# A linear-attention and FP4 feed-forward kernel: eight small adds and the final norm moved to ScalarE, and the turn's order rearranged on four engines

## The chip, the cores and the metric

One core of one Trainium2 chip runs the kernel. The metric is device time in microseconds (us), from launch to end; lower is better. Each kernel is run several times and its median counts. A profile of one execution gives the start and the length of every instruction on the engines: PE (TensorE), DVE (VectorE), ACT (ScalarE), POOL (GpSimd), and SP, the queue that issues the DMAs.

## The reference, cut to what matters

```
x = L0_attn_x                                  # (32, 256, 128), float32
q, k, v = (x @ W).reshape(b, s, 64, 64)        # for Wq, Wk, Wv
q = relu(q) * 64 ** -0.5 ;  k = relu(k)
kv  = einsum('bsid,bsjd->bsdj', k, v)
out = einsum('bsid,bsdj->bsij', q, kv)         # 64 x 64 for each token
out = out / (einsum('bsid,bsd->bsi', q, k.sum(axis=2)) + 1e-6)
x = layernorm(x + out.reshape(b, s, 4096) @ Wo + bo)
g, u = fp4_linear(x, w_gate), fp4_linear(x, w_up)
x = layernorm(x + fp4_linear(silu(g) * u, w_down))
# fp4_linear rounds both operands in blocks of 16 to the grid
# 0, .5, 1, 1.5, 2, 3, 4, 6, scaled by the block's largest magnitude over 6
```

The attention is within one token, across its 64 heads.

## The kernel before, in words

The 8192 tokens are cut into 64 tiles of 128. `run_tiles` runs 68 turns, and each turn works on five tiles at different stages: turn n projects v, k and q of tile n (`front`), attends for tile n-1 (`attend`), multiplies tile n-2 by Wo (`mid`), does the first layernorm, the gate and up products and the quantisation of tile n-3 (`back`), and the down product and the second layernorm of tile n-4 (`end`). Every float32 operand of a large matmul is split in two bfloat16 halves, "hi" (a rounded copy, made by ScalarE) and "lo" (what is left, made by VectorE or GpSimd), and each product takes three matmuls (`three`, lines 360 to 362).

The order of the work is written out by hand: each engine has an `iteration(t)`, a list of helpers, and runs its helpers strictly in that order. Between engines stand semaphores, which each helper waits for at its head. So a wait at the head of one helper holds up everything behind it on its engine. What the change touches:

- PE, one turn (lines 462 to 497): v in four chunks of 24 matmuls, a transpose of x, k in four chunks with the transpose of h (`h_transpose`, line 426) before the last, the down product (`down`, line 433, which waits for ScalarE's copy `hqT`), then q chunk 0, `out_group` 0, `k_sum` (line 444), `out_group` 1, the transpose of xq (line 451), gate and up (lines 459 and 460), q chunk 1, groups 2 and 3, q chunk 2, groups 4 and 5, two parts of Wo (line 407), q chunk 3, groups 6 and 7 with the rest of Wo. Chunks and groups share three slots of PSUM; each waits until the vector engine has read what was there before.
- `q_bd` is the block-diagonal form of q that the groups load as weights. It is filled by four DMAs (`q_move` on SP), three copies by ScalarE (`q_stay`, line 564, copies (l=1, a=0), (0, 1), (0, 0)) and one by GpSimd (`q_stay`, line 1096). Group 0 of the next turn waits for all of them. The part l=1 needs all four `q_lo` of the turn.
- The normaliser of a group is column 32 of its PSUM slot. VectorE adds 1e-6 (`norm_o`, line 774), takes the reciprocal (`recip`, line 781, for one or two groups) and multiplies (`scale_o`, line 790) into one of two buffers `o32`; ScalarE rounds that to `o_st` (`o_hi`, line 623), and GpSimd writes the rest (`o_lo`, line 1066). `scale_o(g)` waits for `o_lo(g-2)`. In the same way `q_scale` (line 766), `q_hi` (line 597) and `q_lo` (line 1056) handle q.
- The sum of k over the heads: ScalarE's `k_first`, VectorE's three `k_add` (line 731), then `k_fold` 0, 1 and 2 (line 742), which halve `k_acc` from 1024 to 128 columns, then PE's `k_sum` and ScalarE's `k_sums` (line 577).
- `y` (line 899) is the last layernorm's product on VectorE, (r2 - mean) * rstd; `rstd_2` on GpSimd gives the rstd. `h_back` (line 1115) multiplies the rounded h by its scales on GpSimd.
- `h_scale` (line 923) is a tensor_scalar on a small tile in SBUF, among the steps of the h quantisation on VectorE.

The weights are loaded and split before and in the first turns: `weight_hi` on ScalarE, the loop over "vkq" on VectorE (lines 706 to 715), and Wo's lo half on GpSimd (line 1046).

Of the kernel before, what the change touches and what calls it, by code (L numbers as in the profile page):

```python
# [28 lines left out]
ALU = mybir.AluOpType  # L29
# [3 lines left out]
P = 128  # L33
DIM = 128
# [3 lines left out]
T = 128  # L38
# [81 lines left out]
def attention_ffn(nc, x, wq, wk, wv, wo, bo, w_gate, w_up, w_down, out):  # L120
# [5 lines left out]
    with ctx:  # L126
        def sb(name, shape, dt=F32):
            return ctx.enter_context(nc.sbuf_tensor(name, shape, dt))
# [27 lines left out]
        consts = sb("consts", [P, 5])  # L156
# [10 lines left out]
        ve1, rs1, ve2, rs2 = (sb(v, [T, 1]) for v in ("ve1", "rs1", "ve2", "rs2"))  # L167
# [7 lines left out]
        def slot_cols(u):  # L175
# [46 lines left out]
         s_ve2, s_rs2, s_yo, s_store) = (sem(f"s_{v}") for v in (  # L222
             "hmax hsc hrs hn hm hk ht hs hq hps hqT dn x1b r2 st2 agg2 ve2 rs2 yo store").split())
# [34 lines left out]
        def _(sp):  # L258
# [34 lines left out]
            def iteration(t):  # L293
                if t.mid:
# [208 lines left out]
        def _(act):  # L503
# [16 lines left out]
            weight_hi("q")  # L520
# [85 lines left out]

            def h_step(t):
# [18 lines left out]
            def iteration(t):  # L626
                v_hi(t, 0)
                v_hi(t, 1)
                v_hi(t, 2)
                v_hi(t, 3)  # L630
# [4 lines left out]
                q_stay(t, 1, 0)  # L635
                hq_copy(t)
                q_stay(t, 0, 1)
                q_stay(t, 0, 0)
                k_sums(t)
                if t.is_(1):  # L640
                    down_weights()
                x1_keep(t)
                xq_copy(t)
# [25 lines left out]
        def _(dve):  # L669
# [3 lines left out]
            nc.vector.memset(consts[:, 4:5], 1.0)  # L673
            nc.vector.memset(consts[:, 1:2], EPS_LN).then_inc(s_consts, 1)
# [31 lines left out]
            for k in "vkq":  # L706
# [8 lines left out]
                last.then_inc(s_wlo[k], 1)  # L715

# [53 lines left out]

            def norm_o(t, g):
                if t.attend:
                    dve.wait_ge(s_done["out"], t.o * NG + g + 1)
                    nc.vector.tensor_scalar(nrm[:, g % NR, :], slot_cols(("out", g))[:, :, HALF], EPS_NORM, None,
                                            ALU.add).then_inc(s_nrm, 1)
# [175 lines left out]
            def iteration(t):  # L951
                residual_1(t)
                stats_1(t)
                before_mean_1(t)
                v_lo(t, 0)
                mean_1(t)
                v_lo(t, 1)
                v_lo(t, 2)
                x_one(t)
# [22 lines left out]
                norm_o(t, 1)  # L982
# [8 lines left out]
                norm_o(t, 2)  # L991
                norm_o(t, 3)
# [7 lines left out]
                norm_o(t, 4)  # L1000
                norm_o(t, 5)
# [3 lines left out]
                y(t)  # L1005
# [3 lines left out]
                norm_o(t, 6)  # L1009
                norm_o(t, 7)  # L1010
# [11 lines left out]
        def _(pool):  # L1022
# [21 lines left out]
            nc.gpsimd.memset(vst[1][:, 1, :, :, HALF:VS], 0.0).then_inc(s_clear, 1)  # L1044
            pool.wait_ge(s_whi["o"], 1)
# [34 lines left out]
            def rstd_2(t):  # L1080
                if t.end:
                    rstd(t.e, s_agg2, mv2, ve2, rs2, s_ve2, s_rs2)

            def q_stay(t):
# [78 lines left out]
```

## Time and profile before

| | us |
|---|---|
| runs of the kernel before | 2352.80, 2371.66, 2376.55 |
| their median | 2371.66 |
| the profiled execution: its own time | 2365.52 |
| its span, first to last instruction | 2363.7 |
| mean granted TensorE clock in it | 0.969 |

The span is what the engines' rows cover; some 2 us of the profiled time lie around it. Busy shares over the whole span are averages, so they mix the first turns, 60 steady turns and the last ones. The turn is the unit to read: one list of helpers on each engine.

### The profile page before, as it was taken

The numbers are of one execution on the slowest core, as the hardware profiler recorded it, in microseconds if no ns is written. First come the engines' busy times: TensorE is split into PE (matmuls) and PEld (weight loads), VectorE is DVE, ScalarE is ACT, GpSimd is POOL, SyncE is SP. The second block draws the span as 40 slices with busy tenths as digits, with TensorE's granted clock in tenths as the row PEclk, the third lists the DMA queues.
The fourth block names the chain that finished last, engine by engine and source line by source line (L and its number), as shares of the span: only waits on it lengthen the run. The fifth ranks groups of instructions, "written<-read, shape, count | busy, mean of one in ns | idle before, by whom it ended". The sixth has DMA issues, their size and how long they took to land.

```text
span 2363.7 us, 88235 instructions
## 1 busy us (share of the span) xinstructions
PE 2079.3 (88%) x37963; PEld 1977.0 (84%) x37963; DVE 1937.1 (82%) x3933; ACT 1489.2 (63%) x2634; POOL 1676.8 (71%) x2064
## 2 busy tenths in 40 slices
PE   3799999999898999999989999899889989989975
PEld 3788898888888888888888888889888888888864
DVE  7678888888888888888888888888888888888874
ACT  4566666666666666666666666666666666666651
POOL 3577787777677777777767767678667767767773
PEclk8899999999999999999999999999999999999986
DMA  6366656656655755665665665666665655655651
GB/s 186 83 132 148 135 129 136 147 125 130 148 121 123 152 126 120 149 134 115 147 135 113 147 129 118 148 129 129 138 132 116 147 126 121 148 128 120 147 119 39
DMA packets 523212, 308.29 MB, mean 130 GB/s; under 512 B 275590, under 2 KB 497734, under 8 KB 522310
## 3 DMA queue, kind: packets, MB, share of 16 engines
q1 hardware_dynamic: 522822, 302.65, 59.3%
q8 instruction: 298, 4.88, 0.8%
q14 instruction: 92, 0.75, 0.1%
HBM read 17.38 MB, written 4.19 MB: 9 GB/s over the span
## 4 chain that ended last, share of the span: by engine, by line
PE 46%; POOL 18%; ACT 16%; DVE 13%; issue 6%; DMA 1%; DVEq 0%; ACTq 0%; SPq 0%; POOLq 0%
PE ps L360 11%; ACT q_bd L564 11%; PE ps L362 10%; PE ps L361 10%; PE ps L407 10%; POOL o_st L1066 8%; POOL q_nat L1056 8%; DVE q L766 4%; DVE o L790 3%; ACT q_nat L597 2%; PE ps L444 1%; PE ps L459 1%; ACT hqT L571 1%; DVE v_st L749 1%; PE ps L426 1%
## 5 line engine op out<-in xcount | busy, mean ns | idle before, releaser
L1066 POOL TENSOR_TENSOR o_st<-o,o_st 128x256 bf16<-128x256 f32 x1024 | 662.8, 677 | 75.5 <-ACT o_st L623 73.7
L1056 POOL TENSOR_TENSOR q_nat<-q,q_nat 128x512 bf16<-128x512 f32 x512 | 591.1, 1176 | 60.3 <-ACT q_nat L597 60.1
L360 PE MATMUL ps<-v_st,q_bd 128*128 128x66 bf16 x4096 | 462.9, 200 | 139.5 <-ACT q_bd L564 73.4
L360 PEld LDWEIGHTS ps<-v_st,q_bd 128*128 128x128 bf16 x4096 | 421.3, 115 | 169.9 <-DVE o L790 85.4
L623 ACT CAST o_st<-o 128x256 bf16<-128x256 f32 x1024 | 356.6, 404 | 310.2 <-DVE o L790 308.1
L361 PE MATMUL ps<-v_st,q_bd 128*128 128x66 bf16 x4096 | 459.4, 199 | 0.0
L362 PE MATMUL ps<-v_st,q_bd 128*128 128x66 bf16 x4096 | 458.3, 198 | 0.0
L361 PEld LDWEIGHTS ps<-v_st,q_bd 128*128 128x128 bf16 x4096 | 421.7, 117 | 0.3 <-issue 0.2
L362 PEld LDWEIGHTS ps<-v_st,q_bd 128*128 128x128 bf16 x4096 | 420.1, 116 | 0.0
L597 ACT CAST q_nat<-q 128x512 bf16<-128x512 f32 x512 | 292.0, 617 | 179.0 <-DVE q L766 178.8
L749 DVE TENSOR_TENSOR v_st<-ps,v_st 128x1024 bf16<-128x1024 f32 x256 | 312.4, 1222 | 106.4 <-ACT v_st L540 99.4
L407 PE MATMUL ps<-w_o,o_st 128*128 128x128 bf16 x6144 | 376.2, 220 | 6.0 <-DMA o_st<-swap 6.0
L790 DVE TENSOR_TENSOR o<-ps,rec 128x512 f32<-128x512 f32 x512 | 342.6, 682 | 43.8 <-POOL o_st L1066 38.9
L360 PE MATMUL ps<-xT,w_v 128*128 128x128 bf16 x2048 | 352.1, 221 | 20.6 <-DVE v_st L749 14.6
L564 ACT COPY q_bd<-q_nat 64x2048 bf16<-64x2048 bf16 x192 | 363.5, 1893 | 7.8 <-POOL q_nat L1056 4.6
L360 PE MATMUL ps<-xT,w_q 128*128 128x128 bf16 x2048 | 360.2, 220 | 5.1 <-DVE q L766 5.0
L361 PE MATMUL ps<-xT,w_q 128*128 128x128 bf16 x2048 | 359.9, 220 | 0.0
L362 PE MATMUL ps<-xT,w_q 128*128 128x128 bf16 x2048 | 359.9, 220 | 0.0
L407 PEld LDWEIGHTS ps<-w_o,o_st 128*128 128x128 bf16 x6144 | 351.7, 114 | 7.0 <-DMA o_st<-swap 7.0
L360 PE MATMUL ps<-xT,w_k 128*128 128x128 bf16 x2048 | 352.0, 220 | 5.3 <-DVE v_st L749 5.3
L361 PE MATMUL ps<-xT,w_v 128*128 128x128 bf16 x2048 | 352.2, 221 | 0.0
L362 PE MATMUL ps<-xT,w_v 128*128 128x128 bf16 x2048 | 352.2, 221 | 0.0
(125 smaller groups left out, 5411.9 us busy)
## 6 DMA issues: line engine op xcount, KB each, us to landing
q_bd<-q_nat SPq DMA_DIRECT2D x256, 256.0 KB, 4.1
swap<-v_st SPq DMA_DIRECT2D x64, 576.0 KB, 6.4
v_st<-v_st SPq DMA_DIRECT2D x64, 576.0 KB, 5.3
v_st<-swap SPq DMA_DIRECT2D x64, 576.0 KB, 5.5
swap<-o_st SPq DMA_DIRECT2D x64, 512.0 KB, 4.3
o_st<-o_st SPq DMA_DIRECT2D x64, 512.0 KB, 8.4
o_st<-swap SPq DMA_DIRECT2D x64, 512.0 KB, 6.0
x_in<-in_L_attn_x SPq DMA_DIRECT2D x64, 64.0 KB, 5.6
```

Of the source, the lines that this page charges most:

```text
L360: nc.tensor.matmul(dst, lhs(0), rhs(0), start=True, stop=False)
L361: nc.tensor.matmul(dst, lhs(0), rhs(1), start=False, stop=False)
L362: return nc.tensor.matmul(dst, lhs(1), rhs(0), start=False, stop=True)
L407: last = nc.tensor.matmul(Y, omat[t.par][:, lo, j // EB, :, j % EB], womat[:, lw, j, :], start=(j == 0 and k == 0), stop=(j == HALF - 1 an ...
L564: nc.scalar.copy(qbd[rows, l, :, a, e:e + HALF, :].rearrange("p k e s -> p k (e s)"), qnat[rows, l, a].rearrange("p k e s -> p k (e s)")). ...
L597: last = nc.scalar.copy(qnat[:, 0, a, :, c * EC:(c + 1) * EC, :], src[:, a])
L623: last = nc.scalar.copy(ost[1 - t.par][:, 0, :, a, g * G:(g + 1) * G, :], src[:, a])
L749: nc.vector.tensor_tensor(lo, slot_cols(("v", c)).rearrange("p e t -> p t e"), hi, ALU.subtract).then_inc(s_read["v"], 1)
L766: nc.vector.scalar_tensor_tensor(out=q32[:, c % QR, :].rearrange("p (e t) -> p e t", t=T), in0=slot_cols(("q", c)), scalar=0.0, in1=ks[:, ...
L790: nc.vector.tensor_tensor(o32[:, g % OR, :].rearrange("p (s b e) -> p s b e", b=2, e=HALF), slot_cols(("out", g))[:, :, 0:PW].rearrange("p ...
L1056: last = nc.gpsimd.tensor_tensor(qnat[:, 1, a, :, e, :], src[:, a], qnat[:, 0, a, :, e, :], ALU.subtract)
L1066: last = nc.gpsimd.tensor_tensor(lo[:, :, a], src[:, a], hi[:, :, a], ALU.subtract)
```

## The change

It has these parts.

1. `norm_o`, eight per turn, goes from VectorE to ScalarE, as an activation with the 1e-6 as a per-partition bias taken from `consts`. It stands at nine places between ScalarE's copies, and waits there for PE's group and, because of the ring of four, for an earlier `recip`.
2. `y` goes from VectorE to ScalarE, as an activation with scale rstd and bias -mean * rstd. GpSimd works out that bias with two more instructions in `rstd_2`, one of which waits for the rstd. ScalarE does `y` before `q_hi(1)`.
3. On ScalarE the second `q_stay` copy goes ahead of `hq_copy`.
4. On VectorE `x_round` and `x_grid` close up around `k_fold(2)`, and `mean_1` goes ahead of `v_lo(0)`.
5. On GpSimd `q_lo(3)` goes ahead of `o_lo(6)` and `o_lo(7)`, `x_bias` ahead of `q_lo(2)`, and `h_back` from the end of turn n to the head of turn n+1, between `rstd_1` and `q_stay`. GpSimd's `q_stay` waits for `o_lo` and `h_back` too.
6. On SP the two `q_move(1, ...)` go ahead of the first move of `o_st`.
7. In the first turn the split of Wq goes behind the third chunk of v on ScalarE and VectorE, and GpSimd's lo half of Wo waits for the three folds (`s_tree` at 3).

The diff, cut to its core:

```
 # ScalarE
+def norm_o(t, g):
+    if not t.attend: return
+    if not (t.is_(1) and g < NR):
+        act.wait_ge(s_rec, t.o * NG + g + 1 - NR)
+    act.wait_ge(s_done["out"], t.o * NG + g + 1)
+    nc.scalar.activation(nrm[:, g % NR, :], slot_cols(("out", g))[:, :, HALF], ACT.Identity,
+                         bias=consts[:, 6:7]).then_inc(s_nrm, 1)
+def y(t):
+    if t.end:
+        act.wait_ge(s_store, 16 * (t.e + 1))
+        act.wait_ge(s_nb, t.e + 1)
+        nc.scalar.activation(y_out[:, :], r2[:, :], ACT.Identity, bias=nb[:, 0:1],
+                             scale=rs2[:, 0:1]).then_inc(s_yo, 1)
 ...
                 o_hi(t, 1)
+                norm_o(t, 2)
+                norm_o(t, 3)
+                y(t)
                 q_hi(t, 1)
 ...
                 o_hi(t, 5)
+                norm_o(t, 6)
                 q_hi(t, 3)
+                norm_o(t, 7)
                 o_hi(t, 6)
 # GpSimd
             def rstd_2(t):
                 if t.end:
                     rstd(t.e, s_agg2, mv2, ve2, rs2, s_ve2, s_rs2)
+                    nc.gpsimd.tensor_tensor(nm[:, :], mv2[:, 0:1], consts[:, 5:6], ALU.mult).then_inc(s_nm, 1)
+                    pool.wait_ge(s_rs2, t.e + 1)
+                    pool.wait_ge(s_nm, t.e + 1)
+                    nc.gpsimd.tensor_tensor(nb[:, :], nm[:, :], rs2[:, :], ALU.mult).then_inc(s_nb, 1)
 ...
                 rstd_1(t)
+                h_back(t)
                 q_stay(t)
 ...
+                x_bias(t)
                 q_lo(t, 2)
                 o_lo(t, 4)
                 o_lo(t, 5)
-                x_bias(t)
+                q_lo(t, 3)
                 o_lo(t, 6)
-                h_back(t)
                 o_lo(t, 7)
-                q_lo(t, 3)
 # GpSimd, before the turns
+            pool.wait_ge(s_tree, 3)
             pool.wait_ge(s_whi["o"], 1)
             nc.gpsimd.tensor_tensor(w_o[:, 1, :], stage["o"], w_o[:, 0, :], ALU.subtract).then_inc(s_wlo["o"], 1)
```

On ScalarE, this is the stretch from `k_first` to the copy of xqT in a steady turn, before. `q_bd<-q_nat` are the `q_stay` copies, `hqT<-ps` is `hq_copy`, `ks<-ps` is `k_sums`.

```order
L552 ACTIVATE k_acc<-ps 128x1024
L564 COPY q_bd<-q_nat 64x16x128
L571 COPY hqT<-ps 128x128 x2
L571 COPY hqT<-ps 96x128
L564 COPY q_bd<-q_nat 64x16x128 x2
L577 COPY ks<-ps 128x128
L582 COPY x1b<-x 128x128
L587 COPY xqT<-ps 128x128
```

And the same stretch in the changed kernel, where line 613 is `norm_o`:

```order
L552 ACTIVATE k_acc<-ps 128x1024
L564 COPY q_bd<-q_nat 64x16x128 x2
L571 COPY hqT<-ps 128x128 x2
L571 COPY hqT<-ps 96x128
L564 COPY q_bd<-q_nat 64x16x128
L613 ACTIVATE nrm<-ps,consts 128x8
L577 COPY ks<-ps 128x128
L582 COPY x1b<-x 128x128
L613 ACTIVATE nrm<-ps,consts 128x8
L587 COPY xqT<-ps 128x128
```

Two copies of q stand ahead of the copy of hqT now instead of one, and a norm ahead of ks and another ahead of xqT.

On VectorE, this is the stretch of the folds, before. `nrm<-ps` is `norm_o(0)`, `xq<-xm,xq` is `x_round`, `xq<-xq,xm` is `x_grid`.

```order
L742 TENSOR_TENSOR k_acc<-k_acc 128x512
L863 SCALAR_TENSOR_TENSOR xm<-xm,consts 128x128
L742 TENSOR_TENSOR k_acc<-k_acc 128x256
L774 TENSOR_SCALAR nrm<-ps 128x8
L742 TENSOR_TENSOR k_acc<-k_acc 128x128
L870 TENSOR_TENSOR xq<-xm,xq 128x128
L781 RECIPROCAL rec<-nrm 128x8
L875 TENSOR_TENSOR xq<-xq,xm 128x128
```

And in the changed kernel, where lines 774 and 807 are the fold and the reciprocal:

```order
L774 TENSOR_TENSOR k_acc<-k_acc 128x512
L889 SCALAR_TENSOR_TENSOR xm<-xm,consts 128x128
L774 TENSOR_TENSOR k_acc<-k_acc 128x256
L896 TENSOR_TENSOR xq<-xm,xq 128x128
L774 TENSOR_TENSOR k_acc<-k_acc 128x128
L901 TENSOR_TENSOR xq<-xq,xm 128x128
L807 RECIPROCAL rec<-nrm 128x8
```

The norm, which waits for group 0 on PE, no longer stands between the second and the third fold, and the first reciprocal comes behind the whole of the x quantisation.

## Rows read from the trace of the kernel before

**Rows 1.** Timeline of DVE, line 899: start, length, instruction; of 60 rows three.

```profile
202.50 0.70 DVE L899 SCALAR_TENSOR_TENSOR y_out<-r,mv,rs 128x128 f32<-128x128 f32 x1
...
1251.76 4.21 DVE L899 SCALAR_TENSOR_TENSOR y_out<-r,mv,rs 128x128 f32<-128x128 f32 x1
...
2282.14 0.67 DVE L899 SCALAR_TENSOR_TENSOR y_out<-r,mv,rs 128x128 f32<-128x128 f32 x1
```

**Rows 2.** Two turns from y to y: busy of PE, PEld, DVE, ACT, POOL; clock; DMA.

```profile
270.93:305.04 34.11, 31.62 (x597) 30.34 (x595) 28.61 (x63) 23.06 (x41) 25.91 (x33) 1.00 0.64 137
1251.76:1288.68 36.92, 32.59 (x586) 30.55 (x584) 31.67 (x62) 22.96 (x41) 25.92 (x33) 0.95 0.60 126
```

**Rows 3.** Timelines of POOL and PE beside the long y of rows 1.

```profile
1254.54 1.29 POOL L1066 TENSOR_TENSOR o_st<-o,o_st 128x256 bf16<-128x256 f32 x2
...
1256.63 0.22 PE L360 MATMUL ps<-v_st,q_bd 128*128 128x66 bf16 x1 [1.79 <-DVE o L790]
```

**Rows 4.** Timeline of PE in a short turn; in brackets the idle time before and its releaser.

```profile
287.80 0.89 PE L433 MATMUL ps<-w_dn,hqT 128*128 128x128 f32 x6
288.53 0.22 PE L360 MATMUL ps<-xT,w_q 128*128 128x128 bf16 x1
...
291.16 0.22 PE L360 MATMUL ps<-v_st,q_bd 128*128 128x66 bf16 x1 [1.12 <-ACT q_bd L564]
...
292.60 0.38 PE L444 MATMUL ps<-k_acc,both 128*128 128x128 f32 x1 [0.46 <-DVE k_acc L742]
...
294.48 0.54 PE L459 MATMUL ps<-w_gu,xqT 128*128 128x352 f32 x1 [0.45 <-ACT xqT L587]
...
300.49 0.22 PE L360 MATMUL ps<-v_st,q_bd 128*128 128x66 bf16 x1 [0.32 <-DVE o L790]
```

**Rows 5.** Timeline of ACT in the same turn.

```profile
284.57 1.88 ACT L564 COPY q_bd<-q_nat 64x2048 bf16<-64x2048 bf16 x1
286.67 0.59 ACT L571 COPY hqT<-ps 128x128 f32<-128x128 f32 x3 [0.21 <-PE ps L426]
287.28 3.82 ACT L564 COPY q_bd<-q_nat 64x2048 bf16<-64x2048 bf16 x2
```

**Rows 6.** Timeline of DVE in the same turn: the folds.

```profile
289.98 0.68 DVE L742 TENSOR_TENSOR k_acc<-k_acc 128x512 f32<-128x512 f32 x1
...
292.18 0.17 DVE L774 TENSOR_SCALAR nrm<-ps 128x8 f32<-128x8 f32 x1 [0.98 <-PE ps L362]
292.27 0.28 DVE L742 TENSOR_TENSOR k_acc<-k_acc 128x128 f32<-128x128 f32 x1
```

**Rows 7.** Groups by line: busy us, mean ns of one, idle before.

```profile
L774 DVE TENSOR_SCALAR nrm<-ps 128x8 f32<-128x8 f32 x512 | 68.5, 157 | 103.1 <-PE ps L362 103.1
L577 ACT COPY ks<-ps 128x128 f32<-128x128 f32 x64 | 17.1, 267 | 138.1 <-PE ps L444 138.1
L610 ACT ACTIVATE sig<-sig,consts 128x352 f32<-128x352 f32 x64 | 37.6, 587 | 7.0 <-DVE sig L798 7.0
```

**Rows 8.** Timelines of POOL and, last, DVE in the turn of rows 4.

```profile
294.89 0.19 POOL L1072 TENSOR_TENSOR ve<-mv,consts 128x1 f32<-128x1 f32 x1 [1.26 <-DVE mv L893]
...
295.95 2.31 POOL L1056 TENSOR_TENSOR q_nat<-q,q_nat 128x512 bf16<-128x512 f32 x2 [0.24 <-ACT q_nat L597]
298.22 2.56 POOL L1066 TENSOR_TENSOR o_st<-o,o_st 128x256 bf16<-128x256 f32 x4
...
300.88 0.69 DVE L790 TENSOR_TENSOR o<-ps,rec 128x512 f32<-128x512 f32 x1 [0.44 <-POOL o_st L1066]
```

**Rows 9.** The first turn: timelines of POOL, DVE and PE.

```profile
42.64 7.93 POOL L1046 TENSOR_TENSOR w_o<-o_st,w_o 128x4096 bf16<-128x4096 f32 x1 [10.06 <-ACT w_o L523]
...
43.31 8.59 DVE L742 TENSOR_TENSOR k_acc<-k_acc 128x512 f32<-128x512 f32 x3
...
51.95 0.58 PE L444 MATMUL ps<-k_acc,both 128*128 128x128 f32 x1 [8.60 <-DVE k_acc L742]
```

**Rows 10.** Line 923 (`h_scale`): lengths in ns, least, median, greatest.

```profile
L923 DVE TENSOR_SCALAR hsc<-hsc x64: 168/570/716, 162.3 to 2352.1; 128x22 f32<-128x22 f32 x64
```

More of the change, by code:

```diff
@@ L166, in attention_ffn @@
         mv1, mv2 = sb("mv1", [T, 2]), sb("mv2", [T, 2])
-        ve1, rs1, ve2, rs2 = (sb(v, [T, 1]) for v in ("ve1", "rs1", "ve2", "rs2"))
+        small = sb("small", [T, 6])
+        ve1, rs1, ve2, rs2, nm, nb = (small[:, i:i + 1] for i in range(6))
         ps = ctx.enter_context(nc.psum_tensor("ps", [P, 8, 512], F32))
@@ L221, in attention_ffn @@
         (s_hmax, s_hsc, s_hrs, s_hn, s_hm, s_hk, s_ht, s_hs, s_hq, s_hps, s_hqT, s_dn, s_x1b, s_r2, s_st2, s_agg2,
-         s_ve2, s_rs2, s_yo, s_store) = (sem(f"s_{v}") for v in (
-             "hmax hsc hrs hn hm hk ht hs hq hps hqT dn x1b r2 st2 agg2 ve2 rs2 yo store").split())
+         s_ve2, s_rs2, s_nm, s_nb, s_yo, s_store) = (sem(f"s_{v}") for v in (
+             "hmax hsc hrs hn hm hk ht hs hq hps hqT dn x1b r2 st2 agg2 ve2 rs2 nm nb yo store").split())
         PER = {"k": NC - 1, "v": NC, "q": NC, "out": NG}
@@ L293, in iteration @@
             def iteration(t):
+                if t.attend:
+                    sp.wait_ge(s_qlo, (t.n * NC))
+                    q_move(1, 0)
+                    q_move(1, 1)
                 if t.mid:
@@ L605, in sigmoid @@
                     nc.scalar.activation(sig[:, :], TB0[:, 0:FFN], ACT.Sigmoid).then_inc(s_sig, 1)
+            def norm_o(t, g):
+                if not t.attend:
+                    return
+                if not (t.is_(1) and g < NR):
[3 more added lines that the diff above has]
+                                     bias=consts[:, 6:7]).then_inc(s_nrm, 1)
             def h_step(t):
@@ L629, in iteration @@
                 v_hi(t, 2)
+                if t.is_(0):
+                    weight_hi("q")
                 v_hi(t, 3)
@@ L635, in iteration @@
                 q_stay(t, 1, 0)
+                q_stay(t, 0, 1)
                 hq_copy(t)
-                q_stay(t, 0, 1)
                 q_stay(t, 0, 0)
+                norm_o(t, 0)
                 k_sums(t)
@@ L642, in iteration @@
                 x1_keep(t)
+                norm_o(t, 1)
                 xq_copy(t)
@@ L650, in iteration @@
                 o_hi(t, 3)
+                norm_o(t, 4)
+                norm_o(t, 5)
                 q_hi(t, 2)
@@ L704, in _, with weight_lo @@
             nc.vector.tensor_tensor(xT[0][:, 1, :], TB1[:, 0:T], xT[0][:, 0, :], ALU.subtract).then_inc(s_xlo, 1)
-            for k in "vkq":
+            def weight_lo(k):
                 dve.wait_ge(s_whi[k], 1)
@@ L715, in _ @@
                 last.then_inc(s_wlo[k], 1)
+            weight_lo("v")
+            weight_lo("k")
             def down_quantise():
@@ L769, in q_scale @@
                 ).then_inc(s_read["q"], 1)
[L771 to L775, printed above, removed]
             def recip(t, g, count):
@@ L954, in iteration @@
                 before_mean_1(t)
+                mean_1(t)
                 v_lo(t, 0)
-                mean_1(t)
                 v_lo(t, 1)
                 v_lo(t, 2)
+                if t.is_(0):
+                    weight_lo("q")
                 x_one(t)
@@ L973, in iteration @@
                 k_fold(t, 1)
-                norm_o(t, 0)
+                x_round(t)
                 k_fold(t, 2)
-                x_round(t)
+                x_grid(t)
                 recip(t, 0, 1)
-                x_grid(t)
                 stats_2(t)
@@ L1091, in q_stay @@
                 pool.wait_ge(s_qlo, t.n * NC)
+                if t.mid:
+                    pool.wait_ge(s_olo, t.o * NG)
                 if t.back:
-                    pool.wait_ge(s_rs1, t.b + 1)
                     pool.wait_ge(s_x1, t.b + 1)
+                if t.end:
+                    pool.wait_ge(s_hq, t.e + 1)
                 held = qnat[64:128, 1, 1].rearrange("p k e s -> p k (e s)")
@@ L1112, in h_back @@
             def h_back(t):
-                if t.back:
-                    pool.wait_ge(s_hs, t.b + 1)
+                if t.end:
+                    pool.wait_ge(s_hs, t.e + 1)
                     nc.gpsimd.tensor_tensor(blocks(h[:, :]), blocks(h[:, :]), per_block(hsc[:, 0, :], h[:, :]),
```

24 lines of the change are left out of this document (3 added, 21 removed).

## The prediction, as made before the changed kernel ran

> **What bounds the kernel now.** I first listed the starts of one instruction that runs once a turn, y on VectorE. From the first of rows 1 to the last there are 60 of them and 59 intervals: 2282.14 - 202.50 = 2079.6 us, 35.25 each. They are of three kinds, by the length of y. It is near 0.70 us in most turns and 4.2 us in 20 of them [rows 1]. The 20 intervals with a long y at their head average 36.92 us, the 19 behind such a one 34.58, the other 20 34.21; the least is 34.11. (20 x 36.92 + 19 x 34.58 + 20 x 34.21 is 2079.6.) So of 2079.6 us only 59 x 34.11 = 2012.5 are quiet turns, and 67 us hang on the long y or on what follows it.
>
> What the long y waits for is to be seen beside it: y ran from 1251.76 to 1255.97, GpSimd was at work until 1255.83, and y ended 0.14 us after that [rows 1, 3]. It reads r2 and rstd, both in SBUF. Meanwhile group 7's slot was not read and PE stood for 1.79 us [rows 3]. Such a turn also shows a granted clock of 0.95 against 1.00 in the quiet one [rows 2]: after the standstill some of PE's work ran at 1.2 in place of 2.4 GHz.
>
> Then a quiet turn, 34.11 us, in which PE is busy 31.62, VectorE 28.61, GpSimd 25.91 and ScalarE 23.06 [rows 2]. PE's timeline shows what it stands for: 1.12 us for ScalarE's last copy of q_bd, 0.46 for the third fold, 0.45 for xqT, and 0.32 for scale_o(2) [rows 4]; scale_o(3) is late too, since it starts as o_lo(1) of GpSimd ends (300.78, then 300.88) [rows 8]. So PE bounds the turn, with some 2.5 us of short waits in it, and VectorE's own busy time matters only where it is late.
>
> **The change, part by part, in a quiet turn.**
>
> *hq_copy behind the second q_stay.* PE's down product needs hqT. Now it starts at 287.80, and group 0 waits for the last q_stay, which ends at 291.10 [rows 4, 5]. In the new order the copies run at 284.57 and, at the pitch of a pair (3.82 - 1.89 = 1.93), 286.50, to 288.39. hqT follows to 289.02, and the third q_stay to 290.95. PE's down would start at about 289.1, q chunk 0 0.73 later, group 0 another 24 x 0.0556 = 1.34 later: 291.17, where it stood at 291.16. The wait moves from q_bd to hqT and is worth nothing; bounds +0.1, and -0.2 where ScalarE had waited for h's transpose (0.21 us here). I take 0.
>
> *The fold.* The third fold started at 292.27, behind a norm that had waited 0.98 us for group 0 [rows 6]. Without it the chain is set by the down product: its end at 289.99, residual_2 to 290.3, first fold from 290.45, third over at about 292.1. Group 0's issue ends at 291.97, so k_sum starts at 292.13, where it was 292.60: -0.47. The wait of 0.46 [rows 4] is nearly gone. Bounds -0.2 and -0.6. x_grid is over earlier as well, so xq is not late next.
>
> *Norms on ScalarE.* On VectorE one took 157 ns [rows 7]. The nearest rows on ScalarE are a PSUM copy of 128 columns without a per-partition operand, 267 ns, and h_step with one, 587 ns for 352 columns [rows 7]. I take 0.27, bounds 0.2 and 0.4. Eight are 2.2 us of ScalarE a turn and y about 0.5 (bounds 0.3 and 0.6): 23.06 becomes 25.8, which has room. What matters is the place. norm_o(1) waits for group 1 and stands ahead of the copy of xqT; PE's transpose of xq ends only a little behind group 1, so the copy is late by a quarter to a half of a norm: +0.07. norm_o(3) waits for group 3 and with y stands ahead of q_hi(1), which starts about 0.9 late against PE. But its follower q_lo(1) on GpSimd stands behind o_lo(1) anyway [rows 8], by my walk with 0.2 us to spare: 0, and if that cover is gone 0.2 to 0.5. The other norms replace a VectorE step of the same wait: 0.
>
> The Trainium skill speaks against this part. "ScalarE: Activation LUTs", in its rules for kernel authors, gives adds and multiplies to VectorE rather than ScalarE, and under "What ACT_TABLE_LOAD costs" it gives 186 ns, plus 93 for each per-partition operand, plus 0.833 ns a column. By that a norm is 286 ns and y 479 ns. The engine with fewer waits on it is here the better place in spite of the rule, by the rows above, since what goes is a wait on VectorE and not work.
>
> *nm and nb.* Two more instructions of 0.19 us, with a wait, stand ahead of q_lo(0). GpSimd had waited 0.24 us there for q_hi(0) [rows 8]. The rstd starts 0.07 earlier, as a norm is gone ahead of mean_2. Net +0.09 (bounds 0 and +0.25).
>
> *What of it reaches the end of the turn.* PE comes to gate and up 0.47 - 0.07 = 0.40 earlier. Later it waits for scale_o(2) and (3), and (3) hangs on GpSimd: q_lo(0) is 0.47 - 0.09 = 0.38 earlier, and so are o_lo(1) and group 5. Behind that nothing waits long. So a quiet turn is 34.11 - 0.38, say 33.75 us.
>
> *GpSimd's order.* Its work between q_lo(0) and q_stay is the same in sum once nm and nb are counted before it. By my walk through the turn rstd_1 is over 0.8 us before x_one, and h_back ends as x_one starts. x_one reads two SBUF operands, like y; if it is held, it is for at most the 0.8 us of h_back, and PE then waits at k chunk 2. I take 0, bound +0.3 a turn. o_st's first move goes out over a microsecond later, behind q_move(1, ...) on SP, but Wo, which waits for the third one, did not wait in a steady turn. q_move(1, ...) goes out earlier, off the path. mean_1 is off it too.
>
> *y off VectorE.* No instruction that stands long at the meeting with GpSimd is left but h_scale, below. The 20 long turns and the turns behind them become quiet ones. The 20 intervals with no long y near them still averaged 34.21, 0.10 over the least; I keep that. So 59 x (35.25 - 33.85) = 82.6 us less, of which 61 are y and 21 the shorter turn.
>
> *The first turn.* The three folds took 8.59 us beside Wo's lo half (7.93 us on GpSimd), and PE stood 8.60 [rows 9]. Undisturbed, the first and the third take 0.68 and 0.28 [rows 6] and the middle one lies between, 1.4 in all, so 7.2 go. Wq's split no longer stands ahead of v_lo, which puts the folds some 2 us earlier, but then Wo's lo half stands ahead of q_lo(0), and q_scale(2) waits for that. I take -8, bounds -4 and -10. The three or so turns before 202.50 give -1, and the longer chain to the last y +0.5.
>
> **The sum** is made against the profiled execution, 2365.5: 2365.5 - 82.6 - 8 - 1 + 0.5 = 2274.4. That execution is 6 us below the median of the runs, 2371.66. The runs differ by 24 us, which is some 8 long turns, so I expect the changed kernel's runs to lie closer together, and its median where its profile is: **2275 us**, -4.1%.
>
> The page "GPSIMD Engine Reference" of the Trainium skill says in its key points that GpSimd shares its SBUF interfaces with VectorE and contends with VectorE instructions that read two SBUF operands or use a two-port mode. The trace agrees for y (up to 4.2 us), for the folds (8.59 against 1.4 us) and for h_scale (0.57 against 0.17).
>
> **The rivals.**
>
> *Only y counts.* If the norm ahead of xqT, nb, or q_hi(1) eat what the fold gives back, the quiet turn stays at 34.11: 59 x (35.25 - 34.21) = 61, so 2365.5 - 61 - 8 = 2296. For it: PE's waits are chained, and one that goes has often an heir. Against: the fold's 0.46 is followed by nothing as tight but 0.09 of GpSimd.
>
> *The short waits go altogether.* If GpSimd's q_lo(0) moves with the fold and the copy of hqT is quicker than I have it, another 0.4 us a turn: 2275 - 24 = 2251. Against: o_lo(1) is limited by GpSimd's own work.
>
> *h_scale takes y's place (slower).* It is a tensor_scalar from SBUF to SBUF, and it took 570 ns in the median where its least is 168 [rows 10]: it already waits 0.4 us for GpSimd each turn, but has always been let in at the next end of a GpSimd instruction, as y was in two turns of three. With the norms gone from ahead of it, it meets o_lo(0) about 0.05 us later in GpSimd's phase. If it is let in as badly as y, a turn costs 2.8 us (36.92 - 34.11), and scale_o(2) is held behind it. The change's gain of 91 us is used up from 91 / 2.8 = 32 long turns of 59; with all 59 it would be 2275 + 165 = 2440. Against: 0.716 us is its greatest in 64 turns.
>
> *The norms' place.* If ScalarE's queue is late by 0.5 us at q_hi(1) in each turn, and GpSimd with it: 2275 + 30 = 2305.
>
> **Chances.** Forecast (2255 to 2290) 0.52. Only y, or the norms late (2290 to 2348) 0.27. The short waits gone (below 2255) 0.10. h_scale or another meeting with GpSimd 0.11, of which 0.05 ends within 1% of before and 0.06 above. The measurement tells about 1% from no change. So faster 0.89, same 0.05, slower 0.06. The range reaches from the third case to the end of the second's mass: 2245 to 2325.
>
> **What the profile of the changed kernel would show.** Right: turns of 33.6 to 34.0 us with hardly a spread; PE waiting about 1.1 us for hqT at the down product, next to nothing for q_bd and under 0.2 for the fold; o_lo(1) still ahead of group 5; norms near 0.27 us; the first k_sum at about 42 us instead of 51.95. Wrong: turns of 34.1 (a wait took the fold's place; its row would have a releaser on ScalarE or GpSimd), or 33.3 (GpSimd did not hold group 5), or a VectorE instruction of 3 to 4 us on h_scale, x_one or a fold.

## The result, and the profile after

The changed kernel takes 2272.06 us (median of 4, 2269.25 to 2275.05), the kernel before beside it 2373.8 (median of 4, 2352.8 to 2376.55). The ratio is 0.959, interval 0.954 to 0.964. (Ratios, here and below, leave out a kernel's runs that lie more than 1.5% above its fastest.) The forecast was 2275 us, in a range of 2245 to 2325. The profiled execution took 2271.46 us; its span is 2269.7 where it was 2363.7, so 94.0 us went.

Where they went is read first from one instruction that runs once a turn on VectorE, residual_1. This is its source view, before and then after (form, least/median/longest in ns, first and last start).

```profile
L811 DVE TENSOR_TENSOR r<-ps,x_res x64: 278/279/292, 141.1 to 2342.1; 128x128 f32<-128x128 f32 x64
```

```profile
L837 DVE TENSOR_TENSOR r<-ps,x_res x64: 278/281/293, 133.4 to 2245.0; 128x128 f32<-128x128 f32 x64
```

Ahead of the first one 141.1 - 133.4 = 7.7 us are gone. The 63 intervals between took 2201.0 and take 2111.6: 89.4 less. Behind the last one 21.6 us became 24.7: 3.1 more. The sum is 94.0. The intervals of the steady part are 33.5 to 34.2 us, three in four of them between 33.65 and 33.85, and none is long. One such turn in the view by windows (busy of PE, PEld, DVE, ACT, POOL; clock), to be held against the two of [rows 2]:

```profile
1212.73:1246.50 33.77, 31.65 (x597) 30.38 (x595) 27.59 (x53) 25.02 (x52) 26.11 (x35) 1.00 0.65 138
```

PE's work is the same 31.6 us. Nine instructions per turn (eight norms and y) went from VectorE to ScalarE; the counts in the rows differ by one or two more, from instructions cut by the windows' edges. VectorE is busy 1.0 us less than in the quiet turn before, ScalarE 2.0 more. It is 2.0 and not the 2.7 forecast, since an instruction on ScalarE partly overlaps its neighbour in the records. The granted clock is 1.00, with no dip; from 200 to 2180 us it averages 1.00 too, where the kernel before had 0.99.

PE's timeline of the same turn answers to [rows 4] (in brackets the idle time before, and its releaser):

```profile
1225.14 0.94 PE L434 MATMUL ps<-w_dn,hqT 128*128 128x128 f32 x6 [1.08 <-ACT hqT L571]
1225.92 0.22 PE L361 MATMUL ps<-xT,w_q 128*128 128x128 bf16 x1
...
1227.26 0.19 PE L361 MATMUL ps<-v_st,q_bd 128*128 128x66 bf16 x1
...
1228.21 0.38 PE L445 MATMUL ps<-k_acc,both 128*128 128x128 f32 x1
...
1230.16 0.53 PE L460 MATMUL ps<-w_gu,xqT 128*128 128x352 f32 x1 [0.52 <-ACT xqT L587]
...
1236.22 0.22 PE L361 MATMUL ps<-v_st,q_bd 128*128 128x66 bf16 x1 [0.36 <-DVE o L816]
```

Measured from the start of v in the turn, 1212.73 here and 276.63 in [rows 4]:

| PE reaches | before | forecast | after |
|---|---|---|---|
| down product | 11.17 | 12.47 | 12.41 |
| group 0 | 14.53 | 14.54 | 14.53 |
| k_sum | 15.97 | 15.50 | 15.48 |
| gate and up | 17.85 | 17.45 | 17.43 |
| group 4 | 23.86 | not given | 23.49 |
| end of the turn | 34.11 | 33.75 | 33.77 |

The 1.12 us for q_bd became 1.08 for hqT, and the 0.46 for the fold is gone. VectorE in this stretch, against [rows 6]:

```profile
1226.53 0.68 DVE L774 TENSOR_TENSOR k_acc<-k_acc 128x512 f32<-128x512 f32 x1
...
1227.33 0.42 DVE L774 TENSOR_TENSOR k_acc<-k_acc 128x256 f32<-128x256 f32 x1
...
1227.87 0.28 DVE L774 TENSOR_TENSOR k_acc<-k_acc 128x128 f32<-128x128 f32 x1
```

The third fold ends at 1228.15, 0.06 ahead of k_sum. GpSimd at its meeting with q, against [rows 8]:

```profile
1230.42 0.19 POOL L1084 TENSOR_TENSOR small<-mv,consts 128x1 f32<-128x1 f32 x1 [1.52 <-DVE mv L919]
1230.69 0.55 POOL L1086 TENSOR_TENSOR small<-small,consts 128x1 f32<-128x1 f32 x1
1231.21 0.19 POOL L1095 TENSOR_TENSOR small<-mv,consts 128x1 f32<-128x1 f32 x1
1231.55 0.19 POOL L1098 TENSOR_TENSOR small<-small 128x1 f32<-128x1 f32 x1
1231.69 2.30 POOL L1068 TENSOR_TENSOR q_nat<-q,q_nat 128x512 bf16<-128x512 f32 x2
1233.95 2.57 POOL L1078 TENSOR_TENSOR o_st<-o,o_st 128x256 bf16<-128x256 f32 x4
```

Lines 1095 and 1098 are nm and nb. From q_scale(0) to q_lo(0) it was 2.52 us and is 2.66. Measured from the start of v again, q_scale(0) starts at 16.30 us instead of 16.80, q_lo(0) at 18.96 instead of 19.32, and scale_o(3), which waits for o_lo(1), at 23.89 instead of 24.25: 0.36 us earlier, where the forecast had 0.38. The other row to remember is the first: GpSimd sat idle for 1.52 us ahead of rstd_2, and from there it has no gap of size until the end of the turn.

The two operations that moved to ScalarE, and h_scale, the one that could have taken y's place, in their source views:

```profile
L613 ACT ACTIVATE nrm<-ps,consts x512: 253/267/270, 82.6 to 2218.6; 128x8 f32<-128x8 f32 x171
...
L626 ACT ACTIVATE y_out<-r,small x64: 481/483/493, 187.5 to 2267.2; 128x128 f32<-128x128 f32 x64
...
L941 DVE TENSOR_SCALAR hsc<-hsc x64: 178/637/700, 153.8 to 2257.3; 128x22 f32<-128x22 f32 x64
```

y now takes 0.48 us each time. h_scale still waits for GpSimd in nearly every turn, and never for more than 0.70 us.

The first turn answers to [rows 9]:

```profile
41.96 1.48 DVE L774 TENSOR_TENSOR k_acc<-k_acc 128x512 f32<-128x512 f32 x3
44.32 1.22 DVE L798 SCALAR_TENSOR_TENSOR q<-ps,ks 128x1024 f32<-128x1024 f32 x1 [0.88 <-ACT ks L577]
...
53.80 1.23 DVE L798 SCALAR_TENSOR_TENSOR q<-ps,ks 128x1024 f32<-128x1024 f32 x1 [5.42 <-POOL q_nat L1068]
```

The three folds take 1.48 us, and the first k_sum starts at 43.49 us; it had been 51.95, and the forecast was about 42. But Wo's lo half (7.96 us on GpSimd) now stands ahead of q_lo(0), and the third q_scale waits 5.42 us for that.

### The profile page after: what moved, and what is told of

The parts are those of the page before. It is cut to its first block, busy times and chain, and to the rows that moved or that the text cites. A ratio compares the mean times of both kernels' runs of the same rounds, so it can differ in the third digit from the quotient of the medians.

```text
span 2269.7 us, 88816 instructions
## 1 busy us (share of the span) xinstructions
PE 2050.3 (90%) x37963; PEld 1961.0 (86%) x37963; DVE 1805.8 (80%) x3359; ACT 1618.7 (71%) x3210; POOL 1690.7 (74%) x2192
## 4 chain that ended last, share of the span: by engine, by line
PE 55%; POOL 18%; issue 9%; ACT 9%; DVE 6%; DMA 2%; SPq 0%; DVEq 0%; ACTq 0%; POOLq 0%
PE ps L408 15%; PE ps L361 12%; PE ps L363 12%; PE ps L362 12%; POOL o_st L1078 8%; POOL q_nat L1068 7%; ACT q_bd L564 6%; DVE q L798 3%; PE ps L434 3%; DVE o L816 2%; ACT hqT L571 2%; POOL small L1086 2%; PE ps L445 1%; DMA x_in<-in_L_attn_x 1%; ACT ks L577 1%
## 5 line engine op out<-in xcount | busy, mean ns | idle before, releaser
L361 PE MATMUL ps<-v_st,q_bd 128*128 128x66 bf16 x4096 | 456.3, 198 | 42.9 <-DVE o L816 37.5
L362 PE MATMUL ps<-v_st,q_bd 128*128 128x66 bf16 x4096 | 454.0, 198 | 0.0
L363 PE MATMUL ps<-v_st,q_bd 128*128 128x66 bf16 x4096 | 452.5, 197 | 0.0
L361 PE MATMUL ps<-xT,w_v 128*128 128x128 bf16 x2048 | 350.7, 220 | 12.2 <-DVE v_st L781 6.2
L361 PE MATMUL ps<-xT,w_k 128*128 128x128 bf16 x2048 | 352.0, 220 | 0.0
L362 PE MATMUL ps<-xT,w_k 128*128 128x128 bf16 x2048 | 351.9, 220 | 0.0
L363 PE MATMUL ps<-xT,w_k 128*128 128x128 bf16 x2048 | 351.8, 220 | 0.0
L362 PE MATMUL ps<-xT,w_v 128*128 128x128 bf16 x2048 | 350.6, 220 | 0.0
```

The source lines that it names most:

```text
L361: nc.tensor.matmul(dst, lhs(0), rhs(0), start=True, stop=False)
L362: nc.tensor.matmul(dst, lhs(0), rhs(1), start=False, stop=False)
L363: return nc.tensor.matmul(dst, lhs(1), rhs(0), start=False, stop=True)
```

## The experiments

Each kernel ran beside the kernel before on the same chip; its ratio is against that one. The changed kernel itself was run again with the last group of kernels:

> The changed kernel once more, on the same chip as the three that follow: 2272 us, turns of 33.77.

It took 2272.33 us (2270.35 to 2273.55; ratio 0.954, 0.951 to 0.958), 0.3 us from the first job. The four runs of a kernel without long turns lie 1 to 8 us apart, so I compare kernels across the jobs only where they differ by more than some 3 us, and go by the turn below that. All times below are medians of 4 runs if nothing else is said, intervals of ratios stand behind them in brackets, and "turn" is the median interval between residual_1's starts.

**y alone.** The kernel before, with y on ScalarE behind o_hi(1), nm and nb on GpSimd, and all else as it was.

```
 # kernel before
-    y(t)                     # VectorE, SUBTRACT then MULT
+    o_hi(t, 1)
+    y(t)                     # ScalarE, bias=nb, scale=rs2
     q_hi(t, 1)
```

> The kernel before with one part of the change: y on ScalarE (with nm and nb on GpSimd), nothing else. Theory (the meeting of y with GpSimd costs 61 us, the rest of the change 30): no long turns are left, turns of 34.2 us, 2365 - 61 + 5 for nb = 2310 us. Rival (it is VectorE's work that counts, 1.8 us a turn with the norms): y alone takes 0.7 us a turn off VectorE and gives under 20 us, 2345 to 2355, or h_scale takes over the long wait, 2365.

2319.27 us (2317.65 to 2322.34), ratio 0.977 (0.970 to 0.985). The runs lie within 5 us, where the kernel before spread over 44. Its profiled execution, 2317.9, is 48 us below the 2365.5 of the kernel before. The long turns are all gone, and the turn is 34.36 us where the quiet turn was 34.11. Nearly all of that 0.25 is nm and nb: behind the start of v, q_lo(0) starts at 19.55 us, against 19.33 in the quiet turns before, scale_o(3) is later by the same 0.22, and q_hi(1), which now stands behind y on ScalarE, has not moved (21.92 and 21.91). So y is worth the 67 us that hung on the long turns, less 0.25 x 59 = 15 for the two small instructions, less some 4 for turns a little above the median (the mean is 34.43).

**The fold behind group 0.** The changed kernel, with the first reciprocal ahead of the third fold, and the fold ahead of x_round. So the fold waits for group 0 again. It is not quite the order of the kernel before: there only the norm stood ahead of the fold, and the reciprocal behind it.

```
 # VectorE
+    recip(t, 0, 1)
+    k_fold(t, 2)
     x_round(t)
-    k_fold(t, 2)
     x_grid(t)
-    recip(t, 0, 1)
```

> The changed kernel with the first reciprocal put back between the second and the third fold, so that the third fold waits for group 0 again. Theory (the turn is 0.4 us shorter because of the fold): PE waits 0.6 us at k_sum again, turns of 34.2 us, 2272 + 59 x 0.5 = 2300 us. Rival (GpSimd's chain sets the turn and the fold has slack): 2272 to 2278.

2325.5 us (2322.77 to 2326.47), ratio 0.980 (0.972 to 0.987): 53 above the changed kernel, where I expected some 28. PE's waits name it in one line (total, times, longest):

```profile
PE ps L445 <- DVE k_acc L774: 52.6, 64, 1.5
```

52.6 us over 64 turns, 0.82 each: the whole loss is k_sum's wait for the third fold. It is more than the 0.46 of [rows 4], and VectorE's timeline shows why:

```profile
1223.55 0.20 DVE L807 RECIPROCAL rec<-nrm 128x8 f32<-128x8 f32 x1 [0.88 <-ACT nrm L613]
1223.67 0.24 DVE L774 TENSOR_TENSOR k_acc<-k_acc 128x128 f32<-128x128 f32 x1
```

The norm now takes 0.27 us on ScalarE and the reciprocal another 0.2 on VectorE, and both stand between group 0 and the fold. Before, only the norm did, with 0.16 us. So the norm's engine and the fold's place hang together: with the norm on ScalarE a fold behind group 0 costs more than it did, and belongs ahead of the reciprocal.

**The copy of hqT first.**

```
 # ScalarE
-    q_stay(t, 0, 1)
     hq_copy(t)
+    q_stay(t, 0, 1)
```

> The changed kernel with ScalarE's copy of hqT back ahead of the second q_stay copy. Theory (the wait only moves between hqT and q_bd): the down product does not wait, group 0 waits 1.1 us for q_bd, turns within 0.1 us of 33.77, 2266 to 2280. But the folds then hang less on the down product, so a little less is possible where the order lets k_sum go earlier. Rival (the new place of the copy costs or gains on its own): 2300 or 2245.

2265.23 us (2264.23 to 2268.16), ratio 0.955 (0.947 to 0.962); the turn is 33.62. That is 7 us below the changed kernel and the least of all kernels run. PE's wait is again the one for q_bd:

```profile
PE ps L361 <- ACT q_bd L564: 73.3, 64, 2.2
```

The swap of part 3 of the change costs 0.14 us a turn. With the down product earlier, residual_2 and the folds are done earlier too, and k_sum no longer waits for them. In the changed kernel it starts 0.18 us behind the last matmul of group 0 (1228.03, then 1228.21), here 0.04:

```profile
1223.68 0.20 PE L363 MATMUL ps<-v_st,q_bd 128*128 128x66 bf16 x1
1223.72 0.47 PE L445 MATMUL ps<-k_acc,both 128*128 128x128 f32 x2
```

**All norms back on VectorE**, norm_o(0) behind x_grid and the others ahead of their reciprocals.

```
-    nc.scalar.activation(nrm[...], slot_cols(("out", g))[...], ACT.Identity, bias=consts[:, 6:7])
+    nc.vector.tensor_scalar(nrm[...], slot_cols(("out", g))[...], EPS_NORM, None, ALU.add)
```

> The changed kernel with all eight norms back on VectorE (norm_o(0) ahead of the first reciprocal, behind x_grid; the others where they stood); y stays on ScalarE. Theory (it is the place of the first norm among the folds that counts, not the engine): turns of 33.7 to 33.9 us, 2266 to 2280. Rival (taking the norms off VectorE is what shortens the turn): 34.1 us and more, 2293 or above.

2274.31 us (2273.36 to 2274.64), ratio 0.963 (0.960 to 0.965); the turn is 33.83. So the engine of eight norms is worth 0.07 us a turn once the fold stands clear of them. It is the difference of two things: gate and up come 0.09 us earlier, as no norm stands ahead of xqT, but q_lo(0) comes 0.08 later.

**The start undone.** Wq's split ahead of the third chunk of v, and no wait for the folds on GpSimd.

```
 # ScalarE and VectorE: weight_hi("q") and weight_lo("q") back ahead of the turns
 ...
 # GpSimd, before the turns
-            pool.wait_ge(s_tree, 3)
             pool.wait_ge(s_whi["o"], 1)
```

> The changed kernel with the first turn as before: Wq split ahead of v's copies on both engines, and Wo's lo half not held for the folds. Theory: the folds of the first turn take some 8.6 us beside Wo's lo half again, 2272 + 8 = 2280, steady turns unchanged at 33.77. Rival (what the first turn saves is given back in the second): 2272 to 2274.

2274.36 us (2272.91 to 2280.56), ratio 0.963 (0.960 to 0.966). The profiled execution took 2280.56 us, 9 more than the changed kernel's, and its timelines show the old collision of VectorE's first fold with Wo's lo half:

```profile
43.33 7.93 POOL L1055 TENSOR_TENSOR w_o<-o_st,w_o 128x4096 bf16<-128x4096 f32 x1 [10.30 <-ACT w_o L524]
44.32 7.50 DVE L774 TENSOR_TENSOR k_acc<-k_acc 128x512 f32<-128x512 f32 x1
```

The other three runs took 2273.21, 2272.91 and 2275.5, which isn't clear of the changed kernel's own 2269.25 to 2275.05. So the mechanism is there, but in most runs its worth is some 2 us at most and not 8. In the three profiles with the old start (before, y alone, this one) GpSimd begins only 0.7 to 1.0 us ahead of the fold, so another execution may have them the other way round; that is not shown. Whether the collision was absent or its cost was made good later in those three runs stays open.

**y back on VectorE, all else changed.** First as it was, then as a tensor_scalar, which reads one tensor from SBUF and two per-partition operands (the second form is shown).

```
 # VectorE, behind scale_o(t, 4)
+    nc.vector.tensor_scalar(y_out[:, :], r2[:, :], mv2[:, 0:1], rs2[:, 0:1], ALU.subtract, ALU.mult)
 # GpSimd: nm and nb removed
```

> The changed kernel with y back on VectorE between scale_o(4) and scale_o(5), without nm and nb; the norms stay on ScalarE. Theory: y meets GpSimd's o_lo(3) and q_lo(2) again, but x_bias now stands between them; long turns come back in a third of the turns, 2272 + 55 = 2327, at most 2440 if it is held in each turn. Rival (the long y came from the old order of GpSimd, which is gone): 2265 to 2275, with y at 0.7 us or less throughout.

> The kernel with y back on VectorE at the place that gave long turns (2338 us), but as a tensor_scalar with two per-partition operands, so that it reads one SBUF tensor instead of two. Theory A (what reads two SBUF tensors is held long, a tensor_scalar is let in at GpSimd's next end as h_scale is): y under 0.8 us, turns of 33.63, 2265. Theory B (any VectorE instruction that meets GpSimd at this place, ahead of an instruction of GpSimd that waits for nothing, is held until GpSimd pauses): long turns of 36.8 as often as there, 2320 to 2360.

The first took 2337.61 us in the median, with runs of 2368.92, 2321.62, 2318.43 and 2353.6; the second 2336.83 (median of 8, 2311.3 to 2360.67). The ratios are 0.977 (0.966 to 0.989) and 0.987 (0.982 to 0.992); the medians of all runs give 0.980 and 0.990. So either kernel is 65 us above the changed one, and its runs spread over 50 us again. In the profiled executions the quiet turn of the first is 33.63 us, 0.14 less than the changed kernel's, since nm and nb are gone. But y is long in 29 of its first 60 turns, where I expected a third of them, and in 21 of the second's:

```profile
L917 DVE SCALAR_TENSOR_TENSOR y_out<-r,mv,small x64: 341/706/4648, 192.7 to 2364.8; 128x128 f32<-128x128 f32 x64
```

```profile
L917 DVE TENSOR_SCALAR y_out<-r,mv,small x64: 335/635/4577, 196.2 to 2335.0; 128x128 f32<-128x128 f32 x64
```

One long y of the first kernel on VectorE, and GpSimd beside it:

```profile
1320.53 4.64 DVE L917 SCALAR_TENSOR_TENSOR y_out<-r,mv,small 128x128 f32<-128x128 f32 x1
```

```profile
1318.51 2.57 POOL L1079 TENSOR_TENSOR o_st<-o,o_st 128x256 bf16<-128x256 f32 x4
1321.05 0.44 POOL L1120 TENSOR_TENSOR x_res<-x_res,bo_b 128x128 f32<-128x128 f32 x1
1321.46 2.31 POOL L1069 TENSOR_TENSOR q_nat<-q,q_nat 128x512 bf16<-128x512 f32 x2
1323.74 1.28 POOL L1079 TENSOR_TENSOR o_st<-o,o_st 128x256 bf16<-128x256 f32 x2
1326.60 1.31 POOL L1079 TENSOR_TENSOR o_st<-o,o_st 128x256 bf16<-128x256 f32 x2 [1.58 <-ACT o_st L632]
```

y starts within the last instruction of o_lo(3), and is still there when x_bias and the two instructions each of q_lo(2) and o_lo(4) have run. GpSimd ends at 1325.02 and y at 1325.17. It was passed over at five ends of GpSimd's instructions, and let in at the sixth. The last row says why there was a pause there at all: GpSimd's next instruction waits for ScalarE's o_hi(5), and that for scale_o(5), which stands behind y on VectorE. So the hold ended only when GpSimd had run out of work that does not hang on y. A second tensor operand isn't needed for the hold. What else the two forms share, or whether the tensor_scalar is held for a reason of its own, these two runs don't separate; it ended 0.08 us behind GpSimd and the first form 0.15.

**GpSimd's and SP's order back**: x_bias, h_back and q_lo(3) at their old places on GpSimd, q_move(1, ...) behind o_st's first move on SP.

```
 # GpSimd
-    h_back(t)
     q_stay(t)
 ...
-    x_bias(t)
     q_lo(t, 2)
 ...
-    q_lo(t, 3)
     o_lo(t, 6)
+    h_back(t)
     o_lo(t, 7)
+    q_lo(t, 3)
```

> The changed kernel with the order of the kernel before on GpSimd (x_bias, h_back and q_lo(3) at their old places) and on SP. Theory (this part moves only work that has slack): 2266 to 2280. Rival (q_lo(3) early, or h_back out of the end of the turn, is worth a share of the gain): 2290 or above.

2268.52 us (2267.65 to 2272.03), ratio 0.960 (0.957 to 0.963); the turn is 33.76, as in the changed kernel. Parts 5 and 6 of the change together are worth nothing in a turn. Behind the last residual_1, 22.3 us follow here, 24.6 in the changed kernel in both its profiles, and 21.6 in the kernel before. So 2.3 of the 4 us are a price that the new order pays in the last turns, and the rows of the changed kernel show it. h_back now runs at the head of GpSimd's turn, where x_one meets it: x_one takes 0.86 us in the last three turns, where its greatest is 0.35 with the old order. And behind the last x_one residual_2 waits 1.73 us for the down product, which needs h_back:

```profile
L855 DVE SCALAR_TENSOR_TENSOR x<-r,mv,small x64: 340/342/865, 139.1 to 2246.8; 128x128 f32<-128x128 f32 x64
2250.48 0.29 DVE L906 TENSOR_TENSOR r<-ps,x1b 128x128 f32<-128x128 f32 x1 [1.73 <-PE ps L434]
```

The rest of the 4 us lies ahead of the first residual_1, which starts at 131.2 us here. In the changed kernel's two profiles that is 133.4 and 135.9, so this part is not clear of the spread.

**rstd_2 late.** nm and nb cost 0.25 us a turn ahead of q_lo(0). So I put rstd_2 with them behind o_lo(1), and y on ScalarE behind q_hi(2).

```
 # GpSimd
-    rstd_2(t)
     q_lo(t, 0)
     o_lo(t, 0)
     q_lo(t, 1)
     o_lo(t, 1)
+    rstd_2(t)
```

> The changed kernel with GpSimd's rstd_2 (four small instructions) behind o_lo(1) instead of ahead of q_lo(0), and ScalarE's y two helpers later, behind q_hi(2). Theory (GpSimd's start of q_lo(0) sets group 5 and with it the turn; nm and nb cost 0.25 us there): q_lo(0) starts 0.15 to 0.2 us earlier, as soon as q_hi(0) is over, turns of 33.6, 2262. Rival (the path through GpSimd has slack): turns of 33.77, 2272.

2328.93 us (2327.73 to 2330.36), ratio 0.978 (0.975 to 0.982): 57 more than the changed kernel, where I expected less time. The turn is 34.70. GpSimd's timeline:

```profile
1228.67 2.31 POOL L1068 TENSOR_TENSOR q_nat<-q,q_nat 128x512 bf16<-128x512 f32 x2 [2.66 <-ACT q_nat L597]
1230.94 2.57 POOL L1078 TENSOR_TENSOR o_st<-o,o_st 128x256 bf16<-128x256 f32 x4
1233.46 0.20 POOL L1084 TENSOR_TENSOR small<-mv,consts 128x1 f32<-128x1 f32 x1
...
1234.59 0.19 POOL L1098 TENSOR_TENSOR small<-small 128x1 f32<-128x1 f32 x1
1234.73 2.31 POOL L1068 TENSOR_TENSOR q_nat<-q,q_nat 128x512 bf16<-128x512 f32 x2
```

And VectorE, which waits for it:

```profile
1238.41 0.69 DVE L816 TENSOR_TENSOR o<-ps,rec 128x512 f32<-128x512 f32 x1 [1.84 <-POOL o_st L1078]
```

q_lo(0) begins only 0.13 us sooner behind q_scale(0), 2.53 us against 2.66. But some 1.2 us of small instructions (1233.46 to 1234.73) have left an idle slot of GpSimd, which is now 2.66 us long, and entered its unbroken run. scale_o waits for them, and the turn is 0.93 us longer.

That GpSimd's run sets the rest of the turn is seen best over all kernels. These are starts behind the start of v, medians of steady turns (of the quiet ones in the kernel before), in us:

| | q_lo(0) | q_lo(1) | scale_o(3) | turn |
|---|---|---|---|---|
| before | 19.33 | 24.12 | 24.27 | 34.11 |
| y alone | 19.55 | 24.34 | 24.49 | 34.36 |
| the changed kernel | 18.95 | 23.75 | 23.89 | 33.77 |
| norms back | 19.03 | 23.81 | 23.96 | 33.83 |
| the copy of hqT first | 18.82 | 23.61 | 23.76 | 33.62 |
| y back, quiet turns | 18.83 | 23.61 | 23.76 | 33.63 |
| rstd_2 late | 18.90 | 24.96 | 23.84 | 34.70 |

In the first six, each 0.1 us at q_lo(0) is 0.1 us at scale_o(3) and in the turn: from scale_o(3) to the end of the turn it is 9.84 to 9.88 us in all of them. In the last, the small instructions stand between o_lo(1) and q_lo(1), so scale_o(3) isn't late but q_lo(1) is, by 1.21 us, and most of that reaches the end. In a turn GpSimd is busy 26.1 of 33.8 us, and no row of waits by PE names it; it stands behind the rows that name VectorE's o.

**Three edits together**: the copy of hqT first, the orders of GpSimd and SP back, and rstd_2 late. And **the down product late**: the orders back and rstd_2 late, PE's down product behind q chunk 0 and residual_2 behind x_grid, the copy of hqT as in the changed kernel.

```
 # PE, second kernel
-    down(t)
     project(t, "q", 0)
+    down(t)
```

> The changed kernel with three things altered: hqT's copy back at its old place, GpSimd's and SP's order as before, rstd_2 late. If the gains of the three add up (7, 4 and 10 us): 2251. If the first and the third are the same slack in GpSimd's chain: 2258.

> GpSimd's and SP's order as before, rstd_2 late, hqT's copy as in the changed kernel; PE does the down product behind q chunk 0 instead of ahead of it, and VectorE's residual_2 goes behind x_grid. Theory (the wait for hqT can hide behind q chunk 0): PE waits under 0.3 us for hqT and q_bd together less than before, group 0 0.2 us earlier, the fold no longer behind the down product: 2245 to 2255. Rival (all of ScalarE's four copies set group 0 in any order): as the kernel with three alterations, 2251 to 2262.

2321.24 us (2316.68 to 2321.77; 0.974, 0.970 to 0.978), and 2293.96 (2291.87 to 2296.08; 0.964, 0.960 to 0.967). So the gains did not add up as expected, since rstd_2 late is a loss. The first kernel is 8 below rstd_2 late alone: 6.5 between the first and the last residual_1, as the copy gave by itself (6.3), and 2.3 behind the last one, as the old orders gave. The second is 27 below the first, 0.40 us a turn. The first waits 73.2 us in all for q_bd at group 0 and 7.4 for hqT. In the second the wait for hqT is 9.5 (67.5 in the changed kernel), and that for q_bd is

```profile
PE ps L361 <- ACT q_bd L564: 39.8, 64, 1.4
```

So the down product behind q chunk 0, with residual_2 moved along, looks worth 0.4 us a turn, in a kernel that carries the 0.93 of rstd_2 late. With rstd_2 in its place it was not tried, nor was the copy of hqT first together with the old order of GpSimd and nothing else. Of part 4 of the change, mean_1 ahead of v_lo(0) was not run by itself.

## Why the prediction was right

*y off VectorE* was the main term, and its mechanism holds. I took 61 us for it. The trace of the kernel before has 67 on the long turns and those behind them; the move alone gave 48, the rest of the 67 going to nm and nb, and undoing it in the changed kernel cost 65. nm and nb are 0.25 us a turn in the kernel before (y alone) and 0.14 in the changed one (y back on VectorE, quiet turn 33.63 against 33.77). I had 0.09 for them, with a bound of 0.25.

*The fold.* k_sum was forecast 0.47 us earlier in the turn and came 0.49 earlier. Undoing it cost 0.82 us a turn, since the norm's move makes the old order dearer. That isn't the term's worth, but what I hadn't seen: the two parts depend on each other.

*hq_copy behind the second q_stay* I took at 0, within -0.2 and +0.1. It costs 0.14, just outside. The step that failed is "the wait moves from q_bd to hqT and is worth nothing". I followed it only to group 0, which indeed starts at 14.53 in both. But the chain of the folds starts at the down product. My own walk for the fold began there ("its end at 289.99", with the down product late), so it had the price of the copy in it, and I booked it to no part. With the copy in its old place k_sum starts at 15.35 us, 0.62 and not 0.49 earlier than before.

*The norms.* 0.267 us where I took 0.27; the wait for xqT grew from 0.45 to 0.52, as forecast by 0.07. y took 0.483 where I took 0.5. "ScalarE: Activation LUTs" of the Trainium skill would have given, by "What ACT_TABLE_LOAD costs", estimates of 0.286 and 0.479 us; the measured y agrees within 1%, the norm is 7% shorter. Its rule that adds and multiplies belong on VectorE is neither borne out nor refuted by much here for the norms, at 0.07 us a turn for eight of them. For y it would have been wrong here: its move alone gave 48 us, because of what it met on VectorE and not because of its own length.

*GpSimd's and SP's order* I took at 0, and it is 0 in a turn. x_one is held by h_back as I had considered, but only in the last turns.

*The reach to the end of the turn.* 34.11 - 0.38 was forecast, 33.77 measured, and by the way forecast: q_lo(0) and scale_o(3) are 0.36 us earlier, k_sum 0.49. The error of the copy does not show in this sum, since its price was already in the walk. Over the 59 intervals from y to y the mean went from 35.25 to 33.78 us, where I had 33.85: 86 us and not 82.6.

*The first turn.* 7.7 us in the profile where I took 8. But in the changed kernel's second profile it is only 5.2 (135.9 instead of 141.1), and undoing it cost 9 in one run and 1 to 3 in three others. So the agreement with 8 is luck in part. *The last turn:* +3.1 where I took +0.5; 2.3 of it comes from the new orders of GpSimd and SP. That the whole came out within 3 us owes something to luck as well: the steady turns gave some 4 us more than forecast and the last turns 2.6 less, and these errors partly cancel.

*The rivals.* Only y: refuted by the turn, 33.77 and not 34.11; the kernel with y alone took 2319 us, and the one with the fold behind group 0 shows the fold's share. h_scale in y's place: its longest is 0.70 us. The norms' place: q_hi(1) does start later, 22.44 us behind the start of v instead of 21.91. But it ends at 1236.29, and q_lo(1) begins at 1236.48, behind o_lo(1), so the cover of 0.2 us that I had counted on was there. The short waits all gone: no, q_lo(0) moved by 0.36 us and not more, and PE still waits 1.08, 0.52 and 0.36 us. And the runs lie within 6 us, as it should be if the spread before was the number of long turns; with y back on VectorE they spread over 50 again.

## What to carry to other kernels

An instruction that takes 0.7 us in most turns and six times that in others is a wait in disguise; look at the other engine at its end, and price the turns with and without it apart. A short wait is worth what it holds up further on, so follow an edit to the end of the chain and not to the next engine's start. Small instructions that stand in an engine's idle slot cost little (here 0.14 us a turn for the two added ones), and 1.2 us of them in its unbroken run cost 0.93 us each turn, even where no wait of PE names that engine.

## What was not expected of the hardware

In these kernels a VectorE instruction that met a running GpSimd instruction in SBUF was let in at one of two times. It was at the end of GpSimd's current instruction (y in 40 of the first 60 turns; h_scale wherever it met one, apart from a few that start within 0.05 us of an end and go with the next, 0.72 us at most), or only as GpSimd went idle. The number of ends passed over was then always the same: four in all 20 long turns before, five in all 29 and 21 of the two kernels with y back, where x_bias stands there too. Each time GpSimd went idle because its next instruction hung on work behind y. The hold came whether or not y read a second tensor. I expected one of these two, not both from turn to turn in the same place: in both, and in nearly all turns, y starts some 0.55 us ahead of the end of o_lo(3). What decides between them no run shows.
